# A fused attention and quantised-FFN block on one core: wide stack loads, ten idle matmuls, a new order of steps

## What is computed

```python
x = x + attn_a(layernorm(x), Wqkv, bqkv, Wo, bo)     # one head of 128, softmax over 256 keys
x = x + ffn(layernorm(x), qweight, scale, zero, bias)  # weight = (int4 - zero) * scale, 512x512
x = x + attn_b(layernorm(x), wq, wk, wv, wo)         # 32 heads of 16, rotary, causal
x = x + ffn(layernorm(x), qweight, scale, zero, bias)
```

```python
o0 = x0 * c - x1 * s
o1 = x0 * s + x1 * c
```

## Time and profile before

| | us |
|---|---|
| median of 3 runs | 269.43 |
| lowest, highest | 269.05, 269.68 |
| the profiled execution | 268.88 |
| its span, first to last instruction | 267.2 |

### The profile page before, as it was taken

How to read it: one execution, slowest core, us unless ns; L and a number is a source line. 1 busy time by engine, 2 the same in 40 slices (tenths; PEclk the granted TensorE clock), 3 DMA queues, 4 the chain that set the end, 5 groups by cost and what they waited for, 6 DMA issues and landing times.

```text
span 267.2 us, 6455 instructions
## 1 busy us (share of the span) xinstructions
PE 253.5 (95%) x2290; PEld 212.3 (79%) x2290; DVE 229.2 (86%) x416; ACT 142.9 (54%) x237; POOL 182.6 (68%) x226
## 2 busy tenths in 40 slices
PE   5988999999999989999999999999999999999993
PEld 1976887798997978987898888788777787777683
DVE  2868969769999997999998877888998999877986
ACT  4456796653463655357371576645353754456430
POOL 3277889999789898875468896358764643555370
PEclk9999999999999999999999999999999999999999
DMA  6999621802463547233423434334635344101103
GB/s 187 332 372 386 218 81 30 247 0 61 118 160 109 150 121 190 83 98 94 139 74 111 123 109 131 106 99 119 159 103 141 102 129 116 42 1 65 56 0 118
DMA packets 52151, 33.94 MB, mean 127 GB/s; under 512 B 5592, under 2 KB 46744, under 8 KB 52120
## 3 DMA queue, kind: packets, MB, share of 16 engines
q1 hardware_dynamic: 52120, 33.54, 41.6%
HBM read 25.00 MB, written 8.39 MB: 125 GB/s over the span
## 4 chain that ended last, share of the span: by engine, by line
PE 60%; DVE 20%; POOL 6%; issue 5%; DMA 3%; SPq 3%; ACT 2%; DVEq 0%; ACTq 0%; POOLq 0%
PE psum L953 10%; PE psum L954 9%; PE psum L955 9%; PE psum L1132 5%; DVE nmax L902 5%; PE psum L1117 4%; PE psum L1047 4%; PE psum L1095 4%; PE psum L1048 4%; PE psum L977 2%; SPq L521 2%; PE psum L1037 2%; PE psum L1119 2%; DVE stats L823 2%; PE psum L1093 2%
## 5 line engine op out<-in xcount | busy, mean ns | idle before, releaser
L902 DVE TENSOR_REDUCE nmax<-psum 128x4 f32<-128x512 f32 (+1 forms) x64 | 59.1, 946 | 4.4 <-PE psum L1095 4.4
L765 ACT ACTIVATE E<-psum 128x1536 f32<-128x1536 f32 x32 | 46.4, 1450 | 30.0 <-PE psum L1119 19.8
L622 POOL TENSOR_SCALAR_AFFINE_SELECT E<-E 128x512 f32<-128x512 f32 x64 | 41.1, 666 | 30.7 <-ACT E L765 30.6
L953 PE MATMUL psum<-XT_lo,wb_hi 128*128 128x256 f32 x128 | 37.5, 293 | 0.7 <-DVE inv_o L918 0.6
L954 PE MATMUL psum<-XT_hi,wb_lo 128*128 128x256 f32 x128 | 36.1, 282 | 0.0
L955 PE MATMUL psum<-XT_hi,wb_hi 128*128 128x256 f32 x128 | 36.1, 282 | 0.0
L629 ACT ACTIVATE parts<-SH 128x512 bf16<-128x512 f32 x32 | 20.1, 627 | 27.4 <-POOL SH L611 19.4
L953 PE MATMUL psum<-wb_lo,XT_hi 128*128 128x256 f32 (+1 forms) x96 | 32.8, 342 | 0.3 <-DVE XT_lo L833 0.2
L955 PE MATMUL psum<-wb_hi,XT_hi 128*128 128x256 f32 (+1 forms) x96 | 30.6, 319 | 0.0
L954 PE MATMUL psum<-wb_hi,XT_lo 128*128 128x256 f32 (+1 forms) x96 | 30.6, 319 | 0.0
L1095 PE MATMUL psum<-QK 128*128 128x128 bf16 x256 | 29.0, 220 | 0.3 <-DVE nmax L902 0.2
(11 more groups left out here) (119 smaller groups left out, 665.1 us busy)
## 6 DMA issues: line engine op xcount, KB each, us to landing
QK<-qk_parts SPq DMA_DIRECT2D x192, 64.0 KB
qk_parts<-parts SPq DMA_DIRECT2D x16, 384.0 KB, 2.9
X<-L_attn_a_x SPq DMA_DIRECT2D x8, 256.0 KB, 6.0
out<-X SPq DMA_DIRECT2D x6, 256.0 KB, 2.2
wb_raw<-L_attn_b_wk SPq DMA_DIRECT2D x1, 1024.0 KB, 10.3
wb_raw<-L_attn_b_wv SPq DMA_DIRECT2D x1, 1024.0 KB, 12.1
wb_raw<-L_attn_b_wq SPq DMA_DIRECT2D x1, 1024.0 KB, 15.2
QK<-mask_rows SPq DMA_DIRECT2D x8, 128.0 KB
```

The source lines that it names most:

```text
L622: last = nc.gpsimd.affine_select(out=e, in_=e, compare_op=ALU.is_ge, fill=0.0, base=0, pattern=[[0, GH], [1, P]], channel_multiplier=-1)
L765: nc.scalar.activation(E[:, n % 2], bank(3, 3), ACT.Exp, scale=float(HD) ** -0.5).then_inc(done[k], 1)
L902: nc.vector.tensor_reduce(nmax[:, u % 2, g::NG, t], (bank(1, 2) if t else bank(0)).rearrange("p (h k) -> p h k", h=GH), AX, ALU.max, negat ...
L953: nc.tensor.matmul(out_, stat[0], mov[1], start=first, stop=False)
```

## The change

**The loads.** A unit's stacks are filled by six loads, three for queries and three for keys, of 48, 32 and 16 rows. For that a part's rows are laid out in the order (d, head) and not (head, d): the host permutes the columns of wq and wk, the tables of sine and cosine follow, and the swap of RO goes to the partition eight away and not to the neighbour. Each row is then one piece of 4 KB in DRAM where it was eight of 512 B. The bytes stay the same, 768 KB a unit. A wide load of queries writes the same part two or three times; the one of keys writes different parts. The rows of the parts in a stack are interleaved, for queries and keys alike.

**The head.** `("KP", 10)` for `("KP", 8)`, and another order of loads and first products.

**The order.** All 1032 steps are placed anew; apart from KP they are the same steps. CS comes after 12 matmuls of QA instead of 27. The first projection, `("PJ", 0, 0)`, has the same PE steps ahead of it as before.

```diff
+LOADS = ((0, 3), (3, 2), (5, 1))
...
-    pair = (np.arange(P) % HD) // 2
-    sign = np.where(np.arange(P) % 2 == 0, -1.0, 1.0).astype(np.float32)
+    place = np.arange(P) // UH
+    pair = place // 2
+    sign = np.where(place % 2 == 0, -1.0, 1.0).astype(np.float32)
...
-    ("D", "xt", 1, 0), ("XH", 1, 0), ("XL", 1, 0), ("D", "wqkv", 1), ("QH", 1), ("D", "wqkv", 0), ("QH", 0), ("KP", 8),
+    ("D", "wqkv", 1), ("QH", 1), ("QL", 1), ("D", "wqkv", 0), ("QH", 0), ("QL", 0), ("D", "xt", 0, 0), ("KP", 10),
+    ("XH", 0, 0), ("D", "xt", 1, 0), ("D", "wqkv", 2), ("XH", 1, 0), ("QH", 2), ("XL", 0, 0), ("QA", 0, 1, 0),
...
-            return 16 * (2 + (2 * len(Q_PARTS) + 1) * (u // QK_SLOTS) + 2 * len(Q_PARTS))
+            return 16 * (2 + (2 * len(LOADS) + 1) * (u // QK_SLOTS) + 2 * len(LOADS))
...
-                    for a, (stack, which) in enumerate(((queries(u), Q_PARTS), (keys(u), K_PARTS))):
-                        for row, c in enumerate(which):
-                            sp.dma_start(stack[row * HD:(row + 1) * HD],
-                                         scratch[u % 2, c, a].rearrange("(h d) t -> d h t", d=HD)
-                                         ).then_inc(qk_loaded[u % QK_SLOTS], 16)
+                    for row, n in LOADS:
+                        q, kk = (stack[row * HD:(row + n) * HD].rearrange("p h t -> p (h t)")
+                                 for stack in (queries(u), keys(u)))
+                        part = scratch[u % 2, Q_PARTS[row], 0].rearrange("(d h) t -> d (h t)", d=HD)
+                        sp.dma_start(q, part.unsqueeze(1).to_broadcast((HD, n, UH * S))
+                                     ).then_inc(qk_loaded[u % QK_SLOTS], 16)
+                        sp.dma_start(kk, scratch[u % 2, 0:n, 1].rearrange("c (d h) t -> d c (h t)", d=HD)
+                                     ).then_inc(qk_loaded[u % QK_SLOTS], 16)
...
-                    nc.vector.stream_shuffle(SH[:, u % 2], ps, [i ^ 1 for i in range(32)])
+                    nc.vector.stream_shuffle(SH[:, u % 2], ps, [i ^ UH for i in range(32)])
...
+    for n in ("L0_attn_b_wq", "L0_attn_b_wk"):
+        arrays[n] = np.ascontiguousarray(arrays[n].reshape(C, KT, UH, HD).transpose(0, 1, 3, 2).reshape(C, C))
```

## The result

The changed kernel takes 265.25 us (median of 4 runs, 263.90 to 265.80) against 269.24 for the kernel before on the same chip: ratio 0.9846, interval 0.9824 to 0.9869. Two later sets of runs gave 264.01 and 264.09. It is faster, by 1.5 to 1.9%, and the forecast was 265.6. How well its parts hold is another matter. The profiled execution took 265.8 us, its span is 264.1.

What follows compares the result with a forecast made beforehand. TensorE, busy 95% of 267.2 us, was taken as the bound, with VectorE also pacing 60 to 100 us. Head 3.0, middle 0.5 and tail 0.3 sum to 3.8 us off, giving 265.6 us, range 263.6 to 267.3.

Steps and rivals of the forecast that it cites:

- the loads' saving is spent by the order: Stack loads: issuing 2.7 to 4.0 us shorter, mostly used up by 3 to 4 us less PE work before the scores.
- The issues, 0.46 us each: Stack loads on SyncE: each of six wide loads issues in 0.46 us like the old ones, 2.8 us a unit.
- The sum of 5.1 us for issue and landing: Stack loads of a unit: six issues and the landing together take 5.1 us, against 7.9 to 9.2 if slow.
- the rival's own sum: Wide stack loads as slow as twelve: a loss once issue and landing exceed about 7 us; 270.3 us, chance 0.08.
- The middle, 0.5 us: All units' attention stretch: fewer waits on loads gain 0.5 us, bounds a loss of 2 and a gain of 2.5.
- The head, 3.0 us: Start up to the first projection: earlier first product, no hole, sooner fast pace gain 3.0 us, bounds 1.0 and 3.5.
- the slow-clock case: Head: if the fast pace had not come before 10.3 us, QT 0 at 15.2 and the lead 2.4 us.
- the clock rival: Head: the fast clock comes no sooner than before, 0.7 us less lead, 266.3 us; chance 0.15, inside the range.
- The tail, 0.3 us: Last products: VectorE doing the 128-column split before the 384-column one saves 0.3 us, bounds 0 and 0.4.
- The lead was not swallowed: Rival in the middle: full VectorE uses up the head's lead, leaving 268.6 us; chance 0.10 with near misses.
- Slow loads: Rival: six wide stack loads last as long as twelve, costing 4.7 us, 270.3 us in all; chance 0.08.

Runs made afterwards that it cites:

- the loads alone: Kernel before, with its own order and eight idle matmuls, given the six wide loads and their row layout: 268.99 us, ratio 0.9995.
- old head: Changed kernel with the steps ahead of its first projection in the order of before, ten idle matmuls kept: 266.66 us, ratio 0.9906.
- again: The changed kernel unaltered, with ten idle matmuls, measured and profiled a second time: 264.01 us, ratio 0.9813.
- the last set: The changed kernel unaltered, measured and profiled a third time: 264.09 us, ratio 0.9811.
- the loads in blocks: Changed kernel with each wide load taking 16 rows of one part, then 16 of the next, instead of alternating parts: 364.57 us, ratio 1.3557.
- The order alone: Changed order of steps and ten idle matmuls, with the twelve loads, layout and rotary tables of before: 277.38 us, ratio 1.0292.
- twelve loads that lie apart: Changed kernel with each wide load cut into 16-row loads of 4 KB rows, mostly filling every second or third stack row: 298.44 us, ratio 1.1107.

## Why the prediction was right, and where it was not

**What bounds the kernel.** Right. PE is at 96%, and the gain came out of its idle time and, where it held, the pace of the head. That the loads' saving is spent by the order was right too, and stronger than I put it: the loads alone give nothing. The distances I worked out from the two orders hold: from the last projection to the first scores I had 19.6 us for unit 12 and 20.5 for unit 15; after shows 20.3 and 20.6. But two readings under them were wrong. The start of unit 15's scores in before was not a wait on a load: the waits of the earlier trace rows are at units 6 and 7, and of PEld. So its 2.35 us are no landing time; at unit 6 it was 1.9. And the 0.6 us were no time of PE's matmuls.

**The issues, 0.46 us each: wrong.** Five of the six take 0.58 to 0.64 us and the last 0.42, 3.6 us with the gaps and not 2.8. The step that failed is that every issue costs about the same; the pattern of rows matters. The sum of 5.1 us for issue and landing failed with it: at unit 0 the DMA engines are done 5.1 us after the first issue, but in the two profiles in which unit 15 shows when the loads were usable it took 6.9 and 7.2. By the rival's own sum about 7 us would have turned the gain into a loss. It did no harm, since the order leaves just enough: in the first profile the issues of unit 15 start at 218.61, the scores at 225.8, 7.2 us later, and PE doesn't wait.

**The middle, 0.5 us: mis-sized.** It is 1.7 (old head), 1.8 (after), 2.3 (again) and 1.9 us (the last set) by the steps' starts. I had counted only the seen waits on loads. In fact about 2.1 of the 3.8 us of PE idle time in the two middle stretches have gone. My upper bound of 2.5 had been worked out from just these stretches, and was nearer than the value that I took. The waits that went are the first four of before shown above, 2.9 us, against 1.3 us of new ones, and all were for DVE or ACT. With the new loads in the old order they stay; with the old head ahead of the new order they are gone. So the middle's gain is the order's, and the loads only allow it.

**The head, 3.0 us: too large, and for partly wrong reasons.** The lead at PJ(0,0) is 1.3 us in the first profile, 2.2 and 2.9 in the next two of the same kernel, and 2.6 to 3.3 in the six other kernels with this head and ten idle matmuls. The first product comes at 6.6 to 7.8, not 6.2, and the hole did not close: I put the landing of 512 KB at 5.2 us on a line through two landings of before, but the small piece of x_transposed is usable at 5.7 to 6.8. The ten idle matmuls end at 5.7 to 6.4. That costs little, since later loads pace the head: QT 0 starts at 14.9 to 15.6 where the pace held (forecast 14.5, with 15.2 as the slow-clock case), QT 1 at 20.6 to 21.4 (forecast 20.0), and the first projection at 48.9 to 49.9 (forecast about 49). Where the pace falls back, QT 0 is at 16.9. That is the clock rival, priced at 0.7 us and worth 1 to 1.5: I had priced slow matmuls that stay as in before, not ones that start anew behind the new hole.

**The tail, 0.3 us: wrong.** PV(15,0) and the last product have the same lead to 0.02 us. The wait of the earlier trace rows is still there, 0.46 us from row to row instead of 0.57, as the short split now waits for ACT:

```profile
248.72 0.40 PE L963 MATMUL psum<-wb_hi,XT_hi 128*128 128x512 f32 x1
249.18 0.50 PE L961 MATMUL psum<-wb_lo,XT_hi 128*128 128x512 f32 x1
```

```profile
248.84 0.76 DVE L841 TENSOR_TENSOR XT_lo<-O,XT_hi 128x128 fp32r<-128x128 f32 x2 [0.38 <-ACT XT_hi L637]
```

I had taken the long split ahead of it for the cause and not asked when ACT's half would be ready.

**The rivals.** The lead was not swallowed: the first scores of unit 0 keep it to within 0.6 us in every run of the new order but that with the loads in blocks. Slow loads did not occur, but the price was far too low. I gave 4.7 us to loads that last as long as twelve; the runs show 10 to 13. I had counted five late units and halved their lateness, since being late at one unit gives the next one time. The order alone shows seven such waits, of 9.5 us in all, and in the run with twelve loads that lie apart the chain runs through SP's queue. On the transfer itself the rule that I had weighed (the Trainium skill, "DMA: Bandwidth & Descriptors", Specifications: full rate from 512 B) agrees with the runs: twelve loads took 276.0 us with rows of 4 KB and 277.4 with 512 B, and most of that difference is no more than these two vary.

So the total was met with a head too large by 0.8 to 1.7 us in the first two profiles and a middle too small by 1.3 to 1.8. That the two errors cancel to 0.35 us of the measured 265.25 is luck.

## What to carry to other kernels

A tightly planned order and the transfers it was planned with are one change: each alone here gave 0% and -3%, together +1.5 to 1.9%. Where many small transfers are issued from one queue, count the queue's issue time per round, and look at how the rows lie before you look at their length. When two dimensions of a transfer can be swapped, put the one divisible by sixteen outside; the busy share of the DMA engines tells at once if it isn't.

## What was not expected of the hardware

- Twelve issues on SP come, gaps included, to 0.45 to 0.46 us each for 16 neighbouring rows, whether of 512 B or 4 KB, and to 0.62 where most lie two or three rows apart, as much as for 32 or 48 rows of several parts. The spacing is not the whole rule: the change's last load of queries, 16 neighbouring rows, took 0.58 us and the load of keys behind it 0.42. Why is open.
- With its six loads the DMA engines are busy for 1.0 of the time at 180 to 220 GB/s (69 to 71 us); the twelve short ones left them at 0.5 at 144, and twelve of 4 KB neighbouring rows at 0.53 at 148 (69 to 70 us each). So it is the wide loads that do it and not the long rows; that more rows are under way at once is a guess.
- The same first loads are usable at 6.19 to 6.70 us in three executions of the changed kernel and at 5.66 to 6.84 over all eleven of the new head. The pace behind a hole of 1.8 to 1.9 us fell back twice out of two, each time costing about 1.5 us at QT 0.
